# Two layers of a modulated transformer on one core: a shared scale in the block quantization, rows three deep, and a new order of all engines and banks

## The reference

```python
h = _layernorm(x) * (1 + ca) + sa
x = x + ga * attention_of_the_layer(h, ...)
h = _layernorm(x) * (1 + cb) + sb
x = x + gb * feed_forward(h, w_gate, w_up, w_down)
```

```python
scale = jnp.maximum(jnp.max(jnp.abs(xb), axis=-1, keepdims=True) / 6.0, 1e-12)
xn = xb / scale
q = _GRID[jnp.searchsorted(_MID, jnp.abs(xn))] * jnp.sign(xn) * scale
```

## Time and profile before

| | |
|---|---|
| median of 3 runs | 1400.71 us (1400.48 to 1400.77) |
| the profiled execution, on the device | 1395.93 us |
| its span, first to last instruction | 1394.0 us |
| busy: PE, DVE, ACT, POOL | 88%, 80%, 76%, 16% |
| granted TensorE clock, mean | 0.957 |
| share of the last-ending chain: PE, ACT, DVE, issue | 67%, 12%, 11%, 6% |
| one turn of the full pipeline | about 77 us |

### The profile page before, as it was taken

The page is one execution under the profiler, slowest core; times in us unless marked ns, Lnnn a source line. Parts: engine busy times, 40 slices in busy tenths (PEclk is TensorE's granted clock), DMA queues, the critical chain, the costliest instruction groups (busy, mean ns, idle before and its releaser), DMA issues.

```text
span 1394.0 us, 18809 instructions
## 1 busy us (share of the span) xinstructions
PE 1228.5 (88%) x5710; PEld 732.2 (53%) x5710; DVE 1121.0 (80%) x1619; ACT 1062.6 (76%) x2849; POOL 222.7 (16%) x286
## 2 busy tenths in 40 slices
PE   5677888989899999989898999989898999979787
PEld 2234364655656564646556564746455555647453
DVE  5848587988989798979889897979798897965424
ACT  5163868889797979798797979797897979786653
POOL 1000202121211103021212111030212112110100
PEclk9888999999999999999999999999999999989899
DMA  4000000000000000000000000000000000000000
GB/s 133 0 0 8 1 1 8 1 16 1 16 1 16 1 15 2 1 16 1 16 1 16 1 16 1 9 8 1 16 1 16 1 16 1 9 1 8 0 8 8
DMA packets 21488, 13.67 MB, mean 10 GB/s; under 512 B 1552, under 2 KB 20624, under 8 KB 21392
## 3 DMA queue, kind: packets, MB, share of 16 engines
q1 hardware_dynamic: 12944, 8.29, 2.0%
q10 hardware_dynamic: 8448, 4.20, 1.0%
HBM read 8.28 MB, written 4.19 MB: 9 GB/s over the span
## 4 chain that ended last, share of the span: by engine, by line
PE 67%; ACT 12%; DVE 11%; issue 6%; POOL 3%; SPq 0%; DMA 0%; ACTq 0%; DVEq 0%; POOLq 0%
PE ps L1105 10%; PE ps L1218 6%; PE ps L1317 4%; PE ps L923 4%; PE ps L1310 4%; PE ps L1184 3%; PE ps L1017 3%; PE ps L1256 3%; PE ps L1013 3%; PE ps L903 3%; PE ps L1257 3%; ACT hq L502 2%; PE ps L977 2%; PE ps L937 2%; POOL rstd_of_a L411 2%
## 5 line engine op out<-in xcount | busy, mean ns | idle before, releaser
L1105 PE MATMUL ps<-wguT,hqcol 128*128 128x352 f32 x512 | 168.2, 470 | 20.4 <-ACT hqcol L676 12.5
L1569 DVE TENSOR_TENSOR_SCAN state<-beta,outer 128x512 f32<-128x512 f32 x128 | 149.2, 1206 | 0.0
L1105 PEld LDWEIGHTS ps<-wguT,hqcol 128*128 128x128 f32 x512 | 93.1, 191 | 78.2 <-issue 24.6
L418 POOL TENSOR_TENSOR var_of_f<-squares_f,eps_sum 128x4 f32<-128x4 f32 x32 | 12.1, 378 | 656.3 <-ACT hq L502 656.3
L1419 DVE SCALAR_TENSOR_TENSOR hid<-hidcol,hid 128x1408 f32<-128x1408 f32 (+1 forms) x68 | 106.2, 1566 | 6.0 <-ACT hidcol L693 5.9
L1218 PE MATMUL ps<-hidcol,wdT 128*128 128x256 f32 (+1 forms) x384 | 92.5, 384 | 0.4 <-ACT hidcol L702 0.4
L1641 DVE TENSOR_TENSOR hid<-th,ps 128x352 f32<-128x352 f32 x128 | 63.3, 512 | 25.2 <-ACT th L684 16.2
L977 PE MATMUL ps<-state,const 128*32 128x512 f32 x256 | 70.9, 831 | 8.8 <-DVE state L1595 8.4
L1595 DVE TENSOR_TENSOR state<-state,qshare 128x1024 f32<-128x1024 f32 x64 | 76.8, 1221 | 2.2
L903 PE MATMUL ps<-const,hq 128*128 128x128 f32 x128 | 34.8, 335 | 48.7 <-ACT hq L492 47.4
L700 ACT ACTIVATE hidcol<-ps 128x512 f32<-128x512 f32 x64 | 38.1, 595 | 51.6 <-PE ps L1184 51.6
(11 more groups left out here) (236 smaller groups left out, 3291.4 us busy)
## 6 DMA issues: line engine op xcount, KB each, us to landing
xa<-in_x SPq DMA_DIRECT2D x16, 256.0 KB, 2.8
out<-xb ACTq DMA_DIRECT2D x16, 256.0 KB, 2.2
const<-in_const SPq DMA_DIRECT2D x1, 848.0 KB, 6.5
state<-in_wmod SPq DMA_DIRECT2D x1, 768.0 KB, 4.5
outer<-in_wqk SPq DMA_DIRECT2D x1, 256.0 KB, 4.5
ex<-in_w_gate_up SPq DMA_DIRECT2D x2, 128.0 KB, 2.6
fw_key<-in_fw_key SPq DMA_DIRECT2D x1, 256.0 KB, 3.0
fw_val<-in_fw_val SPq DMA_DIRECT2D x1, 256.0 KB, 3.8
```

The source lines that it names most:

```text
L1105: t_.matmul(bank(f"f{l}_{'gu'[g]}{t}")[:, 0:I_FF], hqcol[l][:, t * P:(t + 1) * P], wguT[:, l, g, :], start=True, stop=True).then_inc(s_gu[ ...
L1569: return v.tensor_tensor_scan(state[:, m, c, :], beta[:, m, :], src, 0.0, ALU.mult, ALU.add)
```

## The change

The quantization keeps one scale. `back` and its instruction go, the multiplication by the reciprocal takes a constant with its sign turned, and the last multiplication reads `scale`. The blocks' scratch is three rows instead of four. The rows `xa` and `xb` have room for three pairs, and the semaphores of loads and stores are three. The order of steps is new on PE, ACT and DVE, `BANK` is new, and the `freed` waits follow from both. The bodies also start at another place of the turn (`n` in place of `n - 1`), which alone moves nothing in an engine's stream. The semaphores and waits of the banks aside, this is its core:

```diff
-        xa = sb("xa", [P, 2 * NT, H])
-        xb = sb("xb", [P, 2 * NT, H])
+        xa = sb("xa", [P, 3 * NT, H])
+        xb = sb("xb", [P, 3 * NT, H])
...
-                before_last(sp, s_x2mm, i)
+                if i >= 3:
+                    sp.wait_ge(s_x2mm, i - 2)
...
-                    if not (isinstance(i, int) and i < 2):
-                        act.wait_ge(s_out[i % 2], 8 * i - 8 * (i % 2))
+                    if i >= 3:
+                        act.wait_ge(s_out[i % 3], 16 * (i // 3))
...
-                top, scale, inv, back = (scales[:, k, at:at + nb] for k in range(4))
+                top, scale, inv = (scales[:, k, at:at + nb] for k in range(3))
...
-                    v.tensor_scalar(back, top, -put_back, -SCALE_MIN, ALU.mult, ALU.min)
-                    return v.tensor_scalar(scale, top, 1 / 6.0, floor, ALU.mult, ALU.max)
+                    return v.tensor_scalar(scale, top, 1 / 6.0, SCALE_MIN, ALU.mult, ALU.max)
...
-                return v.scalar_tensor_tensor(dst, src, TIE_DOWN, spread(inv, nb), ALU.mult, ALU.mult)
+                return v.scalar_tensor_tensor(dst, src, -TIE_DOWN, spread(inv, nb), ALU.mult, ALU.mult)
```

Two banks and the wait that follows from them (`f1_u0` and `a_zT` are both bank 0 after; before they were 1 and 4):

```diff
                 if t == 0:
-                    freed(pe, s_norm["z0"], j + 2, NT)
-                    freed_at_ends(pe, s_hcol[1], j + 1, SEQ)
-                    freed_at_ends(pe, s_gd[1], j - 1, SEQ)
+                    freed(pe, s_u, j + 2, SEQ)
+                    freed_at_ends(pe, s_gd[0], j + 1, SEQ)
+                    freed_at_ends(pe, s_ag, j, SEQ)
```

More of the change, by code:

```diff
@@ L382, in _ @@
             turns(sp, body)
-            for p in range(2):
-                sp.wait_ge(s_out[p], 8 * PAIRS)
+            for p in range(3):
+                sp.wait_ge(s_out[p], 16 * len(range(p, PAIRS, 3)))
         @block.gpsimd
@@ L1382, in body @@
                 do(b3_1, n - 3, 0)
+                do(a8, n - 1)
                 do(c3, n - 2, 1)
-                do(a8, n - 1)
+                do(a2, n, 0)
+                do(b3_1, n - 3, 1)
+                do(c3, n - 2, 2)
+                do(a3, n, 0)
+                do(b3_1, n - 3, 2)
+                do(b3_1, n - 3, 3)
+                do(b1T_0, n - 1)
+                do(a2, n, 1)
+                do(b1R_0, n - 1)
+                do(a3, n, 1)
+                do(a3b, n, 1)
+                do(c5, n - 2)
+                do(c7x, n - 2)
+                do(layer(b2, 0), n - 1)
+                do(b3_0, n - 1, 0)
+                do(b3_0, n - 1, 1)
+                do(c5n, n - 2)
+                do(b3_0, n - 1, 2)
+                do(b3_0, n - 1, 3)
+                do(c6r, n - 2)
             turns(pe, body)
@@ L1650, in b4 @@
                 w = hid[l].rearrange("p t (b e) -> p (t b) e", e=BLK)
[L1651 removed]
+                scale_blocks(part, w, w, blk[l], 0, NBLK).then_inc(s_hn[l] if part == 3 else s_hch[l], 1)
             def b4q(l, i, part):
@@ L1728, in body @@
             def body(n):
-                do(a2x, n - 1, 0)
-                at_start(weight_blocks, n - 1, 0, 0, 7)
-                do(c4a, n - 3, 0)
-                do(c4a, n - 3, 1)
-                do(a2x, n - 1, 1)
-                at_start(weight_blocks, n - 1, 0, 0, 8)
-                do(layer(b3, 1), n - 4, 0)
-                do(c4b, n - 3)
-                do(a3b, n - 1, 0)
-                at_start(weight_blocks, n - 1, 0, 1, 0)
-                do(c4s, n - 3, 0)
-                do(mean_f0, n - 2)
@@ L1844, in body @@
                 do(layer(b1q, 1), n - 3, 2)
+                do(a2x, n, 0)
+                at_start(weight_blocks, n, 0, 0, 7)
+                do(c4a, n - 2, 0)
+                do(c4a, n - 2, 1)
+                do(a2x, n, 1)
+                at_start(weight_blocks, n, 0, 0, 8)
+                do(a3b, n, 0)
+                at_start(weight_blocks, n, 0, 1, 0)
+                do(layer(b3, 1), n - 3, 0)
+                do(c4b, n - 2)
+                do(mean_f0, n - 1)
+                do(c4s, n - 2, 0)
+                do(c4s, n - 2, 1)
+                do(c4n, n - 2)
+                do(a2p, n, 0)
+                at_start(weight_blocks, n, 0, 1, 1)
+                do(c4v, n - 2)
+                do(a3, n, 0)
+                at_start(weight_blocks, n, 0, 1, 2)
+                do(layer(b3, 1), n - 3, 1)
+                do(layer(b3, 1), n - 3, 2)
+                do(c4p, n - 2)
+                do(layer(b3, 1), n - 3, 3)
+                do(layer(b4, 1), n - 3, 0)
+                do(layer(b1m, 0), n - 1, 0)
+                at_start(weight_blocks, n - 1, 1, 0, 0)
+                do(c4t, n - 2)
+                do(layer(b1m, 0), n - 1, 1)
+                at_start(weight_blocks, n - 1, 1, 0, 1)
+                do(layer(b4, 1), n - 3, 1)
+                do(layer(b1m, 0), n - 1, 2)
+                at_start(weight_blocks, n - 1, 1, 0, 2)
+                do(c4y, n - 2)
+                do(layer(b1m, 0), n - 1, 3)
+                at_start(weight_blocks, n - 1, 1, 0, 3)
+                do(layer(b4, 1), n - 3, 2)
+                do(a2p, n, 1)
+                at_start(weight_blocks, n, 0, 1, 3)
+                do(layer(b1q, 0), n - 1, 0)
+                at_start(weight_blocks, n - 1, 1, 0, 4)
+                do(layer(b1q, 0), n - 1, 1)
+                at_start(weight_blocks, n - 1, 1, 0, 5)
+                do(layer(b1q, 0), n - 1, 2)
+                at_start(weight_blocks, n - 1, 1, 0, 6)
+                do(layer(b4, 1), n - 3, 3)
+                do(a3, n, 1)
+                at_start(weight_blocks, n, 0, 1, 4)
+                do(a4d, n, 0)
+                at_start(weight_blocks, n, 0, 1, 5)
+                do(layer(b4q, 1), n - 3, 0)
             turns(dve, body)
```

508 lines of the change are left out of this document (227 added, 281 removed), and 10 rows, old and new, of the table BANK.

## The result

| | before | after |
|---|---|---|
| median | 1400.74 us (1400.48 to 1401.14, 4 runs) | 1413.74 us (1412.42 to 1417.10, 4 runs) |
| ratio | | 1.0096 [1.0077, 1.0116] |
| the profiled execution | 1395.93 us | 1412.59 us |
| its span | 1394.0 us | 1410.7 us |
| granted TensorE clock, mean | 0.957 | 0.957 |

What follows compares the result with a forecast made beforehand. No engine alone was taken as the limit; PE's waits in two stretches of a turn decide. Terms 0.3 + 0.8 + 0 gave +1.1 us per turn, over 13 turns 14.3 us, added to 1400.7: 1415.0 us, range 1392 to 1429.

Steps and rivals of the forecast that it cites:

- The sum: Whole kernel: +0.3, +0.8 and 0 make +1.1 us per turn, times 13 turns 14.3 us, giving 1415.0 us.
- stretch B: 770 to 797 us of a turn, ending in the first gate product: ACT and DVE chain delays it by 0.8 us.
- Stretch A: 752 to 766 us, b1T_1 to a6: a4 split partly covered, ACT's order delays a6 0.5 us, 0.3 carried on.
- The clock: Rival, chance 0.14: more idle in stretch B lowers PE's clock there, adding 11 us, 1426 in all.
- Stretch B, ACT: On ACT, a3s(0) and b1v_0 moved ahead make the second c4e end later and c4n start 1.2 us later.
- the carry: From stretch A into stretch B: of a6's 0.5 us delay, 0.3 is passed on; bounds 0 and 0.6.
- Stretch B, DVE: On DVE, c4n to the end of b1q_0 takes 14.0 us instead of 14.4; the end comes 0.8 us later.
- Stretch B, PE: On PE, b3_1(0) waits 0.5 us for ucol and a3b(1) (0.96) moves; both covered within the 0.8.
- slower by the chain of B: Main case, chance 0.52: the later ACT and DVE chain up to the first gate product makes the kernel slower.
- The small instruction: On DVE, one TENSOR_SCALAR fewer per quantization saves 0.4 to 0.5 us a turn, 0.2 of it in stretch B's chain.
- Rows three deep: Row loads and stores: the wait that goes was never last, so the price is 0 at both ends.
- The mode change: On PE at the a4 split: by the skill's rule two more tiling-mode changes drain the engine; the trace has no separate row.

Runs made afterwards that it cites:

- e4: Kernel after without the last turn's four table loads, PE's a4(0,0) and a4(0,1) next to each other again: 1396.68 us, ratio 0.9971.
- e9: Kernel before with only the new PE and ACT order of stretch A, the a4 pair kept: 1389.15 us against 1401.40, ratio 0.9917.
- e11: Kernel after without the last turn's four table loads, plus three idle products before b1T_1 in every turn, a4 still split: 1392.82 us, ratio 0.9947.
- e8: Kernel before with three idle products before b1T_1 in every turn, results unused: 1399.55 us, ratio 0.9991.
- e1: Kernel after with ACT's four table loads skipped in the last turn only: 1414.28 us against 1400.55, ratio 1.0101.
- e7: Kernel before with only ACT's new order of stretch B (a3s(0), a8 and b1v_0 moved ahead): 1438.28 us, ratio 1.0272.
- e10: Kernel after without the last turn's table loads, a4 pair put back, ACT's second c4e ahead of b1v_0 again: 1396.26 us, ratio 0.9973.
- e3: Kernel after without the last turn's table loads, ACT's old order of stretch B put back: 1420.86 us, ratio 1.0145.
- e5: Kernel before with only the quantization's one scale, four TENSOR_SCALAR fewer per turn: 1398.23 us against 1400.24, ratio 0.9992.
- e12: Kernel before with stretch A's new order (a4 pair kept), one quantization scale and three idle products before b1T_1 every turn: 1380.23 us against 1400.06, ratio 0.9863.
- e6: Kernel before with only PE's a4(0,0) and a4(0,1) split by b1R_1: 1400.23 us, ratio 1.001.

## Why the prediction was right, and where it was right by luck

**The sum.** 14.3 us were forecast between medians, 13.0 measured; the period was to be 77.9. Six of the twelve periods are 77.8, three are 76.5 and three 78.5 to 78.6. Their mean is 77.68, or +0.74 a turn where +1.1 was forecast, and this makes 8.9 us. What is missing to 13.0 lies in the start and the end, which had no term and scatter by as much between runs. That the sum met the measured time so closely is luck. By its terms: `a6` is 0.53 later in the turn shown and 0.28 in the mean of twelve (10.71 for 10.44), where 0.3 was carried; stretch B costs 0.51, where 0.8 was forecast. The profiled execution was to lie 4.8 us below the median; it lies 1.15 below, so that distance was no constant.

**Stretch A.** Size right in the turn shown, cause wrong. The step said `a1n` at 762.3, that is 7.2 behind `b1T_1`, and `a6` 0.5 later; measured 7.13 and 10.88, +0.53. The times on the way hold too: `c1` was to start at about 760.6, 5.5 behind `b1T_1`, "about the time at which it ran before"; it starts at 5.46, before at 5.66. What failed is what the step made of this. It took the split as covered, since `c1` keeps its time, and put the +0.5 on ACT's order. But `c1` keeps its time because two edits on PE cancel: moved ahead of `a4(1, 0)` it can start at 4.25, as `e4` shows, and the split puts it back by 1.2 when the clock is low. `e9` shows the sign of what is left: the new order of `c1` and `a1n` on both engines, which had been priced at +0.5, brings `a6` forward by 0.5, in `e4` by 0.65. The runs give a simple law. With `a1n` first, in PE's old order, `a6` comes 5.1 us behind it (10.35 less 5.21); with `c1` first it comes 3.75 behind it (10.88 less 7.13, and the same in `e4`, `e9` and `e11`). By these differences the new order gains as long as PE's queue lets `a1n` start before 6.6. The pair gives 5.95, the upper clock 5.57, the split at the lower clock 7.13.

**The clock.** The rival put the danger in stretch B. There it did not fall in the kernel after. It mattered in A instead, where it also falls before, because the change moved the last-ending chain from POOL onto PE (the two chains above). The sum had one call at the lower level in every turn and gave this stretch 0 to 0.6 us. Measured, `a1n` comes at 5.80 in the three turns without a fall, at 7.05 to 7.13 in the six with 3.4 us at the lower level, and at 7.82 to 7.89 in the three with 6.8 us, and `a6` from 0.8 us earlier than before to 1.3 later. This is why the periods after scatter from 76.5 to 78.6. Taking the lower level out is worth 0.7 us by the medians of `e8` and 21.5 us by `e11` against `e1`.

**Stretch B, ACT.** The times are right to the tenth. The second `c4e` was to end 2.1 later by the two moved steps; it ends at 27.88, before at 25.25, of which 0.53 is the carry: 2.10. `c4n` is 1.25 later beyond the carry, forecast 1.2. What a later `a6` costs reaches `c4n` in full: the two are 17.03 us apart in every turn, at either clock. So 0.3 of the 0.5 was too small a carry, and it made up for the 0.8 that was too large. `e7` adds that this order of ACT costs 38 us without the new order and banks of DVE and PE; which of these it needs was not tried.

**Stretch B, DVE.** From `c4n` to the end of `b1q_0` 14.0 us were forecast, before it was 14.4; measured 13.75. The gate product is 1.04 later, forecast 1.1. What the stretch itself costs is 0.5 (gate less `a6`: before 31.82, after 32.33, `e9` 31.81).

**Stretch B, PE.** `b3_1(0)` waits 0.56 (forecast 0.5), and PE takes up `a3b(1)` ahead of `c5`. The prediction held both to be covered ("Both lie within the 0.8"), with the chain over ACT and DVE as the one that sets the gate product. The profile doesn't bear this out: the last-ending chain of B goes over PE, before and after, and after it holds just these two steps. The DVE chain is no better covered, though. Before, PE waited 0.49 us for `wy` ahead of `c5`; after, PE gets there without a wait, 0.15 us behind the end of `wy`, as before, and DVE's `hq` is ready at 729.11 for a `b2_0` that starts at 729.25. Both chains arrive within some 0.1 us of each other, so that neither is shown to be the cause of the 0.5 alone. `e10` took the wait out of the one and gained nothing; `e3` made `ucol` later on the other, and the gate product came 0.53 later behind `a6`. No run puts back `b3_1(0)`'s bank or `a3b(1)`, and the banks and DVE's order were not tried alone. So "slower by the chain of B" is right in its times and open in its cause. And `e4` shows that this part didn't decide the result: with the split taken back and all of B as it is, the kernel is faster than before.

The wait before `b1T_1` is 2.61 (forecast: stays at 2.77), and from the gate product to the next `b1T_1` it is 34.64, before 34.68: the rest of the turn moved nothing, as said.

**The small instruction.** 2.6 us were forecast for two on the chain; 2.0 by the medians of `e5`, not told from nothing. **Rows three deep:** no wait on rows shows in either trace; it was not tried alone.

**The mode change.** By the Trainium skill (TensorEngine Tiling (Array Packing), Tiling Modes) a change of tiling mode drains the engine, so the split would add two drains. The trace shows no row for one. At the upper clock the lone call of `e11` at 683.13 is followed by `c1` at 684.12, a step of 0.99 for 1.05 us of work: no drain of a size that counts. What the split loses is the partner: the same section has different tiles work in parallel, and the pairs of `e4` and `e12` agree (1.94 and 1.16 us for eight records).

**The end.** I had written that starting the bodies at another place of the turn "alone moves nothing in an engine's stream". That was wrong. A step for a pair that doesn't exist issues nothing, but ACT's four table loads belong to no pair and run in every turn, so in the last one they now stand behind the last store. In the trace that is 5.84 less 2.65, 3.2 us; the medians of `e1` don't show it. The Trainium skill (ScalarE: Activation LUTs, What ACT_TABLE_LOAD costs) gives 2.66 us for a switch with its drain; here, with nothing between them, the loads follow every 1.28 us, by which four take 5.1. The 3.2 us are near the 2.7 by which the end is longer than in `e5`, `e6` and `e8`, within a scatter of the same size.

## What to carry to other kernels

Before pricing a reordering, follow the last-ending chain through the stretch and write down which queue each moved step then stands behind. The same split was free while POOL set `a1n`, and cost 17.6 us once PE did and the clock was low. A step that keeps its time may do so because two edits cancel, and then each has a price of its own. Orders of two engines that wait for each other are one edit: taken back singly, both ACT's orders made the kernel slower, and stretch A taken whole made it faster. Where a wait on PE (2.6 to 2.8 us here) brings its clock down just ahead of work on the chain, filling the wait with idle work can be worth more than the whole reordering; where another engine sets the pace, it is worth next to nothing.

## What was not expected of the hardware

Idle products gave back 21.5 us in one order of nearly the same instructions (`e1` to `e11`) and 0.7 us, not told from nothing, in the other (`e8`). Two `a4` calls side by side in different column strips took 1.16 us (`e12`) against 1.05 for one alone at the upper clock, and 1.94 (`e4`) against 1.80 mostly at the lower: the second is nearly free, so a pair that is split costs PE a whole call. Four table loads with nothing in between took 1.28 us each from start to start.
